# Four stages of a decoder reordered, and one sum of keys moved to GpSimd behind a copy by ScalarE

## What is computed

```python
x = x + _L1_attn_ref(_layernorm(x), ...)    # test-time training: two gradient steps per row block, then a group norm
x = x + _L2_xattn_ref(_layernorm(x), ctx_768, ...)   # top 32 of 120 scores, softmax, mean over 4 heads -> FiLM scale and shift
x = x + _L3_attn_ref(_layernorm(x), ...)    # causal attention, 16 heads of 64
x = x + _L3_ffn_ref(_layernorm(x), ...)     # product keys, below, beside a dense feed forward of 512
```

```python
q = q.reshape(b, t, 2, h, n).transpose(2, 0, 1, 3, 4)
sim = jnp.einsum('pbthn,hkpn->pbthk', q, keys)          # 2 sides x 4 heads x 64 keys
scores_xy, idx_xy = jax.lax.top_k(sim, K)               # K = 8
all_scores = (sx[..., :, None] + sy[..., None, :]).reshape(b, t, h, K * K)
scores, pk = jax.lax.top_k(all_scores, K)
w = jax.nn.silu(jnp.einsum('btd,bthkd->bthk', hidden_states, de) * jax.nn.softmax(scores, axis=-1))
```

## Time and profile before

| | us |
|---|---|
| median of 3 runs (lowest, highest) | 4763.19 (4760.88, 4769.77) |
| the profiled execution's own time | 4762.61 |
| its span, first to last instruction | 4760.8 |
| `l1_attn`, from its layernorm to the next stage's | 826 to 1385 |
| `l2_film` | 2091 to 2555 |
| `l3_attn` | 3370 to 3963 |
| `l3_ffn`, to the end | 4240 to 4761 |

### The profile page before, as it was taken

How to read it: one execution, slowest core, us unless ns; L and a number is a source line. 1 busy time by engine, 2 the same in 40 slices (tenths; PEclk the granted TensorE clock), 3 DMA queues, 4 the chain that set the end, 5 groups by cost and what they waited for, 6 DMA issues and landing times. The chain is left out here.

```text
span 4760.8 us, 71373 instructions
## 1 busy us (share of the span) xinstructions
PE 3486.1 (73%) x22142; PEld 2515.3 (53%) x22143; DVE 2834.1 (60%) x8335; ACT 1788.2 (38%) x5180; POOL 676.2 (14%) x867
## 2 busy tenths in 40 slices
PE   3576396555548858558888859999688887867776
PEld 3454296222225635445556646666466664546665
DVE  6455533699967753656662724444566665657775
ACT  1355242111116632135552532222244443436665
POOL 0044532000016762010000200000000000000000
PEclk9788598677767655776665959999899998988888
DMA  4030275000030005130000000000000000000000
GB/s 107 4 150 4 87 233 168 2 0 0 0 126 19 0 1 148 56 84 0 0 0 0 1 9 5 9 9 4 18 0 0 0 0 4 0 14 1 0 0 18
DMA packets 111452, 152.49 MB, mean 32 GB/s; under 512 B 21594, under 2 KB 88216, under 8 KB 109718
## 3 DMA queue, kind: packets, MB, share of 16 engines
q1 hardware_dynamic: 99822, 142.12, 9.6%
q0 software_dynamic: 11520, 9.05, 0.7%
HBM read 107.45 MB, written 58.50 MB: 35 GB/s over the span
## 5 line engine op out<-in xcount | busy, mean ns | idle before, releaser
L1245 PE MATMUL l_attn_p_s<-l_attn_outer,l_attn_upper 128*128 128x512 f32 x256 | 182.3, 877 | 201.9 <-DVE l_attn_outer L1190 121.4
L95 POOL TENSOR_TENSOR rstd<-vareps,minus_half 128x32 f32<-128x32 f32 x11 | 59.8, 5439 | 1527.9 <-DVE vareps L86 1393.6
L398 ACT ACTIVATE l_ffn_sg<-l_ffn_p_g 112x512 f32<-112x512 f32 x192 | 114.6, 597 | 391.9 <-PE l_ffn_p_g L378 368.5
L2582 ACT ACTIVATE l_attn_E<-l_attn_p_s,l_attn_nm 128x128 f32<-128x128 f32 x512 | 182.3, 382 | 157.6 <-DVE l_attn_nm L2545 157.6
L409 DVE TENSOR_TENSOR l_ffn_h<-l_ffn_sg,l_ffn_p_u 112x512 f32<-112x512 f32 x192 | 131.8, 687 | 172.7 <-PE l_ffn_p_u L381 172.1
L1245 PEld LDWEIGHTS l_attn_p_s<-l_attn_outer,l_attn_upper 128*128 128x128 f32 x256 | 70.2, 288 | 302.3 <-issue 178.7
L2979 PE MATMUL l_ffn_p_w<-ident,l_ffn_w 128*128 128x128 f32 x1024 | 157.0, 326 | 89.0 <-DVE l_ffn_w L2864 76.1
L381 PE MATMUL l_ffn_p_u<-l_ffn_f_xTall,l_ffn_wu 128*112 x384 | 198.3, 598 | 8.9 <-DVE l_ffn_h L409 8.9
L2979 PEld LDWEIGHTS l_ffn_p_w<-ident,l_ffn_w 128*128 128x128 f32 x1024 | 151.7, 239 | 97.1 <-DVE l_ffn_w L2864 82.4
L1404 POOL DMA_INDIRECT slots_in<-l_xattn_x,l_xattn_slot x192 | 190.0, 990 | 81.9 <-issue 50.1
L378 PE MATMUL l_ffn_p_g<-l_ffn_f_xTall,l_ffn_wg 128*112 x384 | 198.1, 597 | 0.9 <-DVE l_ffn_al L2423 0.9
(11 more groups left out here) (784 smaller groups left out, 9625.0 us busy)
## 6 DMA issues: line engine op xcount, KB each, us to landing
l_experts_w<-in_L_ffn_w SPq DMA_DIRECT2D x72, 512.0 KB
slots_in<-l_xattn_empty SPq DMA_DIRECT2D x8, 2145.0 KB, 23.9
shares_out<-l_xattn_zero SPq DMA_DIRECT2D x24, 512.0 KB, 13.6
l_combine_got<-shares_out SPq DMA_DIRECT2D x16, 768.0 KB, 4.4
l_attn_toep<-kernel_rows SPq DMA_DIRECT2D x1, 8192.0 KB, 31.6
xattn_toep<-ssm_rows SPq DMA_DIRECT2D x1, 8192.0 KB
l_slots_w<-in_L_ffn_w SPq DMA_DIRECT2D x32, 176.0 KB
l_experts_x<-slots_in SPq DMA_DIRECT2D x72, 65.0 KB
```

The lines of the kernel that those rows point to most:

```text
L398: act.activation(X.sg[:, k % 2], X.p_g[0:X.FP, k % 2], ACT.Silu).then_inc(s.silu_ready, 1)
L1245: mm = pe.matmul(p_s[:, r, a], upper[:], outer[:, r, a * 512:(a + 1) * 512], start=True, stop=True)
L2582: e = act.activation(E[:, u % 2, h], p_s[:, u % 2, odd, c * P:(c + 1) * P], ACT.Exp, bias=nm[:, u % 2, h:h + 1], accum_out=sums[:, u % 2, ...
```

## The change

- `l1_attn`: x is normalised by ScalarE at the start of its iteration, not by VectorE. VectorE reduces the three squares before it adds the output and takes statistics. On TensorE both halves of the projection come before the context's transposes and the output product; ScalarE's copy `cT` moves behind the square `t1`.
- `l2_film`: the mask row is bfloat16 on one partition, with a row of bfloat16 ones, and its matmul moves ahead of the wait for xT. The FiLM products move from the end of an iteration to the start of the next (lag 3), before the transpose of x. VectorE does its FiLM multiply and add after the search, not before it. ScalarE makes four diagonals, then copies xT, then the other four, and takes the FiLM results after that. ScalarE and TensorE start without waiting for the turned scales.
- `l3_attn`: the output product goes into the bank `p_x` and runs before the projection of k, whose copy by VectorE no longer stands before it. The transpose of x moves ahead of the transposes of the weights, and its copy by ScalarE stands between the two halves of the exponentials; the copy of v comes before them.
- `l3_ffn`: `w` has four buffers. ScalarE copies the second item's 256 similarities of side two from PSUM to SBUF (`simy`), and GpSimd makes that item's 2048 sums from the copy. VectorE makes the first item's. `added` for both items stands behind the search for `cut`. On ScalarE silu of the second item, hT, xT and qT come first, then `simy` and the exponentials, between them the copies of the summed heads `wT`. On TensorE the order is: dot and up products, transpose and query product of lag 0, heads of the first item, its dense product, heads of the second item, similarities of lag 0, then the rest of the output products.

```diff
-                    for b, u in item(0):
-                        pair_normalised(R, dve, b, side(xhat[:])).then_inc(s.xhat_ready, 1)
...
+                    for b, u in item(1):
+                        dve.wait_ge(s.sq2_ready, b + 1)
+                        dve.tensor_reduce(st2[:, 0], heads(t2[:]), AX.X, ALU.add).then_inc(s.var2_ready, 1)
+                    for b, u in item(2):
+                        dve.wait_ge(s.sq3_ready, b + 1)
+                        dve.tensor_reduce(gs[:, 1], heads(t3[:]), AX.X, ALU.add).then_inc(s.squares_ready, 1)
+                    for b, u in item(0):
+                        dve.wait_ge(s.sq1_ready, b + 1)
+                        dve.tensor_reduce(st1[:, 0], heads(t1[:]), AX.X, ALU.add).then_inc(s.var1_ready, 1)
...
                     for b, u in item(3):
                         dve.wait_ge(s.xb_ready, b + 1)
                         dve.wait_ge(s.out_psum, b + 1)
...
                     for b, u in item(0):
+                        for r in range(2):
+                            last = act.activation(xhat[:, r * P:(r + 1) * P], row(R.x, b * 2 + r), ACT.Identity,
+                                                  scale=R.rstd[:, bass.ds(b * 2 + r, 1)], bias=R.shift[:, bass.ds(b * 2 + r, 1)])
+                        last.then_inc(s.xhat_ready, 1)
-                    for b, u in item(3):
-                        act.wait_ge(s.ctxT_psum, b + 1)
-                        act.activation(cT[:], p_c[:, 0:W], ACT.Copy).then_inc(s.ctxT_ready, 1)
...
+                    for b, u in item(3):
+                        act.wait_ge(s.ctxT_psum, b + 1)
+                        act.activation(cT[:], p_c[:, 0:W], ACT.Copy).then_inc(s.ctxT_ready, 1)
...
+                    for b, u in item(0):
+                        pe.wait_ge(s.xT_ready, b + 1)
+                        projected(b, 0)
+                    for b, u in item(0):
+                        projected(b, 1)
                     for b, u in item(3):
                         pe.wait_ge(s.ctx_ready, b + 1)
                         for r in range(2):
                             mm = pe.transpose(p_c[:, r * P:(r + 1) * P], qw[u][:, r * P:(r + 1) * P], R.ident[:])
                         mm.then_inc(s.ctxT_psum, 1)
-                    for b, u in item(0):
-                        pe.wait_ge(s.xT_ready, b + 1)
-                        projected(b, 0)
...
-                    for b, u in item(0):
-                        projected(b, 1)
...
-        m4, mneg = sb("m4", [1, NB, SC // 4], U32), sb("mneg", [P, NB, SC])
+        m4, mneg, onesb = sb("m4", [1, NB, SC // 4], U32), sb("mneg", [1, NB, SC], BF16), sb("onesb", [1, P], BF16)
...
-                chain(dve.memset(mneg[:], 0.0))
+                dve.tensor_copy(onesb[:], R.ones[0:1, :])
...
+                    for b, u in item(3):
+                        dve.wait_ge(s.film_done, b + 1)
+                        chain(dve.tensor_tensor(f[:], xr[:, u % 2], p_f[:, 0:P], ALU.mult))
+                        dve.tensor_tensor(row(xin, b), f[:], p_f[:, P:256], ALU.add).then_inc(s.xin_done, 1)
...
-                act.wait_ge(s.scales_ready, 1)
...
+                    for b, u in item(2):
+                        act.wait_ge(s.rz_ready, b + 1)
+                        diagonals(0)
+                        diagonals(1)
+                    for b, u in item(0):
+                        act.wait_ge(s.xT_psum, b + 1)
+                        act.activation(xT[:], p_a[:, 0:P], ACT.Copy).then_inc(s.xT_ready, 1)
+                    for b, u in item(2):
+                        diagonals(2)
+                        diagonals(3).then_inc(s.diag_ready, 1)
...
+                    for b, u in item(3):
+                        if isinstance(b, int) and b == 0:
+                            pe.wait_ge(s.set_ready, 2)
+                            pe.wait_ge(s.scales_ready, 1)
+                        after(pe, s.xin_done, b)
+                        after(pe, s.film_done, b)
+                        pe.wait_ge(s.c_ready, b + 1)
+                        film_of(p_f, slice(0, 256), 1)
+                        film_of(p_g, slice(256, 512), 0)
+                        pe.matmul(p_g[:, 256:384], turn[:], xhat[:, u], start=True, stop=True).then_inc(s.film_psum, 1)
...
+                        for h in range(H):
+                            pe.matmul(p_s[:, h, 0:SC], onesb[:], row(mneg, b), start=True, stop=False, skip_group_check=True)
...
-                        after(pe, s.sc_ready, b)
-                        for h in range(H):
-                            pe.matmul(p_s[:, h, 0:SC], R.ones[:], row(mneg, b), start=True, stop=False, skip_group_check=True)
...
+                    for b, hf, n, u in item(5):
+                        if hf == 1:
+                            dve.wait_ge(s.out_psum, b + 1)
+                            dve.tensor_tensor(row(R.x, b), p_x[:, 0:P], row(R.x, b), ALU.add).then_inc(s.out_taken, 1)
...
+                    for b, hf, n, u in item(2):
+                        act.wait_ge(s.v_psum, n + 1)
+                        act.activation(v[:, u].rearrange("p h e -> p (h e)"), p_x[:], ACT.Copy).then_inc(s.v_ready, 1)
...
+                            for b, hf, n, u in item(1):
+                                if hf == 0:
+                                    act.wait_ge(s.xT_psum, b + 1)
+                                    act.activation(xT[:, u // 2], p_x[:, 0:P], ACT.Copy, scale=gam[:]).then_inc(s.xT_ready, 1)
...
+                        pe.wait_ge(s.v_ready, n + 1)
+                    for b, hf, n, u in item(1):
+                        if hf == 0:
+                            pe.wait_ge(s.xhat_ready, b + 1)
+                            pe.transpose(p_x[:, 0:P], xhat[:, u // 2], R.ident[:]).then_inc(s.xT_psum, 1)
...
+                    for b, hf, n, u in item(5):
+                        if hf == 1:
+                            for c in range(2 * HC):
+                                mm = pe.matmul(p_x[:, 0:P], headsT[:, u - 1 + c // HC, c % HC], wout[:, c], start=(c == 0), stop=(c == 2 * HC - 1))
+                            mm.then_inc(s.out_psum, 1)
                     for b, hf, n, u in item(2):
                         pe.wait_ge(s.q_ready, n + 1)
                         projected(b, hf, u, 1).then_inc(s.k_psum, 1)
-                        pe.wait_ge(s.v_ready, n + 1)
-                    for b, hf, n, u in item(1):
-                        if hf == 0:
-                            pe.wait_ge(s.xhat_ready, b + 1)
-                            pe.transpose(p_x[:, 0:P], xhat[:, u // 2], R.ident[:]).then_inc(s.xT_psum, 1)
-                    for b, hf, n, u in item(2):
-                        pe.wait_ge(s.k_ready, n + 1)
-                    for b, hf, n, u in item(5):
-                        if hf == 1:
-                            for c in range(2 * HC):
-                                mm = pe.matmul(p_y[:, 0:P], headsT[:, u - 1 + c // HC, c % HC], wout[:, c], start=(c == 0), stop=(c == 2 * HC - 1))
-                            mm.then_inc(s.out_psum, 1)
...
+        simy = sb("simy", [P, H * NK])
...
-        w, e_c, e_t = sb("w", [P, PER2, 2, NG_]), sb("e_c", [P, PER2, 2 * H, K * K]), sb("e_t", [P, PER2, 2 * H, K])
+        w, e_c, e_t = sb("w", [P, PER_W, 2, NG_]), sb("e_c", [P, PER2, 2 * H, K * K]), sb("e_t", [P, PER2, 2 * H, K])
...
+                for item in skewed(pool, 3, PAIRS, PER_W):
+                    for b, v in item(1):
+                        pool.wait_ge(s.side_ready, b + 1)
+                        after(pool, s.w_ready, b * 2 - 2)
+                        pool.wait_ge(s.cut_ready, b + 1)
+                        pool.tensor_tensor(sums[:, v % PER2, 1].rearrange("p (h i j) -> p h i j", h=H, i=K),
+                                           xs[:, H:2 * H, 0:K].unsqueeze(3).broadcast_to((P, H, K, NK)),
+                                           simy[:].rearrange("p (h j) -> p h j", h=H).unsqueeze(2).broadcast_to((P, H, K, NK)), ALU.add).then_inc(s.keysum_ready, 1)
...
+                        after(dve, s.keysum_ready, b)
...
+                    for b, v in item(3):
+                        added(b, v, 0)
+                        added(b, v, 1)
+                    for b, v in item(1):
+                        u = v % PER2
+                        dve.tensor_tensor(sums[:, u, 0].rearrange("p (h i j) -> p h i j", h=H, i=K),
+                                          xs[:, 0:H, 0:K].unsqueeze(3).broadcast_to((P, H, K, NK)),
+                                          sim[:, 0, 1].unsqueeze(2).broadcast_to((P, H, K, NK)), ALU.add).then_inc(s.sums_ready, 1)
```

254 lines of the change are left out of this document (127 added, 127 removed).

## The result

The changed kernel takes 4552.34 us (median of 4 runs, 4548.69 to 4555.89) against 4763.02 (4 runs, 4760.88 to 4769.77): ratio 0.9555, interval 0.9539 to 0.9572. That is 210.7 us less; the forecast was 4567, 196 less.

A forecast was written before the change was run, and what follows sets the result against it. Bounds: VectorE in l1_attn, TensorE in l2_film and l3_attn, waits among three engines in l3_ffn. 18 - 98 - 59 - 57 = -196 us gave 4567 us, range 4500 to 4650.

The forecast's parts named there:

- its four terms: Stage forecasts: l1_attn +18 us, l2_film -98, l3_attn -59, l3_ffn -57.
- the edge of the range: l1_attn: upper bound +35 us, if wait and statistics both add and the low clock doubles the products.
- the part that I priced best: l1_attn: VectorE's 1.76 us of output addition and statistics now stand behind the reductions, delaying the gradient.
- 11.3 - 1.7 + 0.3: l2_film, TensorE per sequence: 11.3 us busy, less 1.7 for the float32 mask, plus 0.3 for the bfloat16 one.
- rival 2: TensorE at the upper clock: film bound by VectorE (-125 us), l3_ffn at 24.2 us a pair, kernel 4512 us; chance 0.18.
- The bound of -78: l3_attn: the largest gain allowed, -78 us, if removing TensorE's two waits brings no new wait.
- the middle between 24.2 and 28.5: l3_ffn, us a pair: 24.2 with TensorE at full clock, 28.5 if it idles ahead of groups; 26.3 taken.
- Rival 3: l3_ffn: GpSimd's sum blocks VectorE's masking, up to 4.4 us, and the -57 goes: 4623 us; chance 0.08.
- the ring: l3_ffn: three engines, 63 to 72% busy, hand work around so every wait counts; shortening it gives -57 us.
- Rival 4: l3_ffn: GpSimd's sum becomes the new bound and the kernel slower, 4789 us at 12 ns a column; chance 0.03.
- Rival 1: TensorE at the lower clock: film gains -20 us, l3_ffn stays at 28.5 us a pair, kernel 4674 us; chance 0.20.
- Rival 5: Reorderings don't remove their waits, the next being as long; only mask and xhat count: about 4700 us; chance 0.03.

The follow-up runs named there:

- e3: Changed kernel with l1_attn as before, except that VectorE's three reductions stand ahead of the output's addition and statistics: 4542.12 us, l1_attn 585.6 us.
- e7: Changed kernel with l2_film's mask row float32 on 128 partitions again, in its new place: 4545.90 us.
- e11: Changed kernel with l3_attn's output product back in p_y behind k and its copy, early transpose of x kept: 4628.48 us, l3_attn 590.2 us.
- e5: Changed kernel with GpSimd making each l3_ffn sum twice, first into a tile nobody reads: 4554.55 us in a single execution, stage 458.4 us.
- e10: Changed kernel; in l3_ffn ScalarE's hT, xT and simy precede the second item's silu, and VectorE's sums precede added: 4529.25 us.

## Why the prediction was right, and where it was not

The sum was 15 us too high. Each of its four terms was too small by 11 to 16 us, the loss and the three gains alike: 39 us were missing from the gains and 16 from the loss, so one error hid another.

- **`l1_attn`, +18 against +33.6.** The mechanism is as told, its size is not. VectorE's reduction of `t1` comes every 31.7 us before and every 34.0 after (14 periods each, 878.28 to 1322.03 and 874.97 to 1351.18): 2.3 us a pair where I said 1.4, and 14 periods where I took 13. The part that was too small is the start of the gradient, forecast 1.9 us later and 3.2 later in the mean (7.9 against 4.7). The forecast fits the three iterations at a clock of 0.91 to 0.93; the low clock of the other ten I had only at the edge of the range, and one iteration of before stood for all. `e3` confirms the part that I priced best: 1.76 x 16 = 28, measured 26.
- **`l2_film`, -98 against -109.0.** The period was right: 13.5 us before and 10.25 after in 27 steady steps (the transposes of x from 2132.6 to 2497.4 and from 2164.3 to 2441.0), 3.3 less, forecast 3.2. Two errors hid each other in it. In that stretch TensorE is busy 244.8/27 = 9.1 us, not 9.9, as the clock rose to 0.79 where I left it at 0.66; and it waits 1.2 us, not 0.5. What was missing is the ends: the first transpose comes 4.9 us earlier, forecast 2, and from the last one to the mixing it is 33.3 us instead of 44.0, forecast no change. The mask's four matmuls measure 14.7/29 = 0.5 us, not 0.3. By the earlier trace rows four of 120 columns are 0.36 us if they scale by columns and 0.95 with a fixed half, not 0.25 and 0.8, so my 0.3 lay below both. `e7` shows that the 1.4 us credited to the bfloat16 mask can't be told from nothing once the order is changed, so the term "11.3 - 1.7 + 0.3" names a cause that isn't there. It went towards rival 2, whose -125 should have been 4.0 x 30 + 2 = -122. What I said there of the clock was picked from two rows of four: in the earlier trace rows 0.89 stands at 72% busy beside 0.66 at 83%.
- **`l3_attn`, -59 against -71.6.** The wait left for eT is 14.4/30 = 0.5 us, forecast 0.4 for another copy. The periods are 15.4 us, 2.15 less and not 1.97, and the first and last sequences gain too, which I counted out. (The bound of -78 is 2.37 x 30 = 71.) That each wait could be priced by its own idle time was luck of doing both: `e11` shows that taking only the wait for xT gives 2.7 us.
- **`l3_ffn`, -57 against -72.4.** Steady periods of the changed kernel run from 25.4 to 26.8 us, 26.3 in the mean of eleven, and the forecast was 26.3. That it fits is partly luck. It was the middle between 24.2 and 28.5, and its parts were off: ScalarE waits 49.1/13 = 3.8 us for q where I had 2.1, and 40.2 us in 13.6 pairs, 3.0 a pair, for the heads where I had 1.9. VectorE's wait for silu, which I said would be gone, is 31.8/13 = 2.4 us. The other 15 us are the ends, which I left out: the first and the last of these 13 periods are 23.7 and 24.6 us, and head and tail of the stage are about 10 us shorter together.
- **Rival 3** (0.08) did happen, 3.4 us a pair, and cost nothing: its condition was right and its price wrong, since I charged it to the ring and it lay in VectorE's wait for silu. The rule of the Trainium skill ("SBUF — State Buffer", "Who interferes with whom") holds in every row here: operations with both input tensors in SBUF wait for GpSimd's sum to end (0.49 to 3.43 us in `e5`), those with one of them in PSUM don't (2.27 us beside it in `e10`).
- GpSimd's sum takes 3.6 to 4.2 us, forecast 4.5 from two short additions. Rival 4 is out. Rival 1 is out: the clock rose in the film and stayed at 0.89 in `l3_ffn`. Rival 5 is out, though `e11` shows how near it was in `l3_attn`.

## What to carry to other kernels

Work placed in a wait for another engine is free; the same work moved behind the wait is not, and `l1_attn` paid 26 us for it. When several waits stand in line on one engine, the idle time beside one is a gain only if the next isn't as late: undo the parts one by one before crediting any. Before giving VectorE's work to GpSimd, count VectorE's operations with two inputs in SBUF that fall beside it: here 2.3 us given away brought back 2.1 to 3.4.

## What the runs showed that was not expected

- More work for TensorE cost the film nothing: with 27.7 us more of mask matmuls in 303 us, the granted clock was 0.83 instead of 0.78 and the film took 352.4 us, where ten executions with the bfloat16 mask took 353.2 to 357.6.
- A stage can take another time with no edit to it. The mixing took 185.3 to 185.7 us at a clock of 0.80 in five executions and 190.4 to 190.6 at 0.78 in the others. A stage that is timed together with it can be credited with 5 us that aren't its own.
- A VectorE addition of a few columns (0.22 us for two) took 2.34 us beside GpSimd's sum in `e10`, and a mask of 512 columns (0.74 us) up to 4.11: what is lost depends on when GpSimd ends, not on the size of what is blocked.
